# Writing the gated product of an expert block back into PSUM: one core, a chain of small gated MLPs in split fp32

## The reference

```
x = x + L0(x)                                   # linear + low-rank part
g, u = x @ gate_w, x @ up_w                     # layer 1, for 2 chosen experts and the shared one
x = x + sum_e weight_e * (gelu(g) * u) @ down_w
up, gate = x @ wu.T + bu, x @ wg.T + bg         # layer 2, one chosen expert
x = x + (silu(up) * gate) @ wd.T + bd
x = x + x @ w_bot.T + bias                      # layer 3, a mix of 8 matrices, masked
```

## Time and profile before

| | |
|---|---|
| three runs | 77.83, 78.18, 78.83 us, median 78.18 us |
| span of the profiled execution | 76.4 us from its first to its last instruction |
| TensorE busy | 70.4 us, 92% |
| VectorE busy | 58.6 us, 77% |
| ScalarE busy | 50.0 us, 65% |
| GpSimd busy | 46.3 us, 61% |
| granted TensorE clock | full speed in all 40 slices of the span |

### The profile page before, as it was taken

The page is one execution under the profiler, slowest core; times in us unless marked ns, Lnnn a source line. Parts: engine busy times, 40 slices in busy tenths (PEclk is TensorE's granted clock), DMA queues, the critical chain, the costliest instruction groups (busy, mean ns, idle before and its releaser), DMA issues.

```text
span 76.4 us, 1120 instructions
## 1 busy us (share of the span) xinstructions
PE 70.4 (92%) x303; PEld 54.1 (71%) x303; DVE 58.6 (77%) x93; ACT 50.0 (65%) x94; POOL 46.3 (61%) x48
## 2 busy tenths in 40 slices
PE   4949999799999899999999999999999999999950
PEld 4846788487877567778888788888788687684730
DVE  0165718996999999889987969669989969969940
ACT  5076749477675675577788776767977995736720
POOL 5020048308999999999999999999986300000000
PEclk9999999999999999999999999999999999999999
DMA  0679999999300000000000000000000000000034
GB/s 0 150 235 340 373 324 352 427 425 406 131 3 0 4 0 9 0 0 4 0 0 0 0 0 0 0 0 0 9 0 0 0 0 0 0 0 0 0 137 137
DMA packets 2740, 6.62 MB, mean 87 GB/s; under 512 B 432, under 2 KB 1456, under 8 KB 2736
## 3 DMA queue, kind: packets, MB, share of 16 engines
q1 hardware_dynamic: 2448, 6.18, 22.4%
q10 hardware_dynamic: 288, 0.39, 1.4%
HBM read 6.04 MB, written 0.52 MB: 86 GB/s over the span
## 4 chain that ended last, share of the span: by engine, by line
PE 81%; DVE 9%; DMA 4%; issue 2%; DVEq 0%
PE acc L414 10%; PE gp L410 8%; PE up L414 8%; PE up L410 8%; PE up L411 8%; PE gp L411 8%; PE gp L414 8%; PE acc L410 7%; PE acc L411 7%; DVE hlo L599 4%; DMA condb<-cond 4%; PE gp L521 1%; PE acc L406 1%; DVE wa L612 1%; PE acc L425 1%
## 5 line engine op out<-in xcount | busy, mean ns | idle before, releaser
L599 DVE TENSOR_TENSOR hlo<-h,hhi 128x512 fp32r<-128x512 f32 (+1 forms) x29 | 27.5, 948 | 1.0 <-ACT hhi L333 0.7
L346 ACT ACTIVATE act<-gp 128x512 f32<-128x512 f32 x24 | 14.4, 598 | 14.6 <-PE gp L414 13.3
L267 POOL TENSOR_TENSOR wlo<-raw_skill,whi 128x384 fp32r<-128x384 f32 x16 | 20.1, 1259 | 3.5 <-ACT whi L318 3.5
L333 ACT ACTIVATE hhi<-h 128x512 fp32r<-128x512 f32 (+1 forms) x29 | 17.7, 612 | 3.2 <-DVE h L584 2.6
L591 DVE SCALAR_TENSOR_TENSOR h<-up,gate_w,act 128x512 f32<-128x512 f32 x16 | 12.0, 749 | 4.6 <-ACT act L346 4.2
L414 PE MATMUL acc<-hlo,whi 128*128 128x512 f32 (+1 forms) x28 | 11.6, 415 | 1.0 <-DVE hlo L599 0.8
L410 PE MATMUL acc<-hhi,whi 128*128 128x512 f32 (+1 forms) x28 | 11.3, 402 | 0.0
L411 PE MATMUL acc<-hhi,wlo 128*128 128x512 f32 (+1 forms) x28 | 10.8, 387 | 0.0
L410 PE MATMUL gp<-xhi,whi 128*128 128x512 f32 x27 | 10.7, 397 | 0.1
L410 PE MATMUL up<-xhi,whi 128*128 128x512 f32 x27 | 10.7, 396 | 0.0
L411 PE MATMUL gp<-xhi,wlo 128*128 128x512 f32 x27 | 10.7, 395 | 0.0
(11 more groups left out here) (99 smaller groups left out, 99.3 us busy)
## 6 DMA issues: line engine op xcount, KB each, us to landing
raw_skill<-skill SPq DMA_DIRECT2D x4, 768.0 KB, 8.7
raw_l<-l SPq DMA_DIRECT2D x2, 386.5 KB, 9.2
raw_shared<-shared SPq DMA_DIRECT2D x4, 192.0 KB, 4.2
w3in<-l SPq DMA_DIRECT2D x1, 576.0 KB, 7.6
x<-x_t SPq DMA_DIRECT2D x2, 256.0 KB, 3.8
out_t<-res ACTq DMA_DIRECT2D x1, 256.0 KB, 2.1
params<-l SPq DMA_DIRECT2D x1, 128.0 KB, 2.6
out_t<-res ACTq DMA_DIRECT2D x1, 128.0 KB, 1.7
```

Source lines behind the costliest of these rows:

```text
L267: pool.tensor_tensor(wlo[:, p, :], raw_piece(p), whi[:, p, :], ALU.subtract).then_inc(s_wlo, 1)
L333: sc.activation(hhi[:, i, t], h[:, i, t], ACT.Copy).then_inc(s_hhi, 1)
L346: sc.activation(act[:, k % 2, :], gp[k % PAIRS][:, :], ACT.Gelu_apprx_tanh).then_inc(s_act, 1)
L599: ve.tensor_tensor(hlo[:, i, t], h[:, i, t], hhi[:, i, t], ALU.subtract).then_inc(s_hlo, 1)
```

## The change

The tile `h` goes away. `hidden(k)` writes its product over its own input, the up bank in PSUM, and both `h_hi(k)` and `h_lo(k)` read the product from there. Only the last block, whose halves overlap, keeps an SBUF tile (`h_last`). The up bank is therefore in use until `hlo` is made, so gate_up(k) waits for the low half of block k - 3 where it waited for its product, and the first half-wise down projection, which writes over a part of an up bank, waits likewise. `hidden(k)` no longer waits for the buffers of `h`.

```diff
-        h = sb("h", [P, HBUFS, T])
+        h_last = sb("h_last", [P, T])
...
+        def hidden_of(k, t):
+            return h_last[:, t] if k == N - 1 else up[k % PAIRS][:, t]
...
-                sc.activation(hhi[:, i, t], h[:, i, t], ACT.Copy).then_inc(s_hhi, 1)
+                sc.activation(hhi[:, i, t], hidden_of(k, t), ACT.Copy).then_inc(s_hhi, 1)
...
                 if k >= PAIRS:
-                    pe.wait_ge(s_h, k - PAIRS + 1)
+                    pe.wait_ge(s_hlo, k - PAIRS + 1)
...
                 if is_first(k):
-                    pe.wait_ge(s_h, N1 + 2)
+                    pe.wait_ge(s_hlo, N1 + 2)
...
             def hidden(k, t=slice(0, T)):
-                i = k % HBUFS
                 ve.wait_ge(s_act, k + 1)
                 ve.wait_ge(s_u, k + 1)
-                if k >= HBUFS:
-                    ve.wait_ge(s_hhi, k - HBUFS + 1)
-                    ve.wait_ge(s_hlo, k - HBUFS + 1)
-                a, u = act[:, k % 2, t], up[k % PAIRS][:, t]
+                a, u, out = act[:, k % 2, t], up[k % PAIRS][:, t], hidden_of(k, t)
...
-                    ve.tensor_tensor(h[:, i, t], u, a, ALU.mult).then_inc(s_h, 1)
+                    ve.tensor_tensor(out, u, a, ALU.mult).then_inc(s_h, 1)
...
-                ve.tensor_tensor(hlo[:, i, t], h[:, i, t], hhi[:, i, t], ALU.subtract).then_inc(s_hlo, 1)
+                ve.tensor_tensor(hlo[:, i, t], hidden_of(k, t), hhi[:, i, t], ALU.subtract).then_inc(s_hlo, 1)
```

More of the change, by code:

```diff
@@ L583, in hidden @@
                     c = L2_BLOCKS * PIECE + L2_BLOCKS + j
-                    ve.scalar_tensor_tensor(out=h[:, i, t], in0=u, scalar=raw_l2[:, b, c:c + 1], in1=a,
+                    ve.scalar_tensor_tensor(out=out, in0=u, scalar=raw_l2[:, b, c:c + 1], in1=a,
                                             op0=ALU.add, op1=ALU.mult).then_inc(s_h, 1)
                 elif expert_of(k) is None:
-                    ve.tensor_tensor(h[:, i, t], u, a, ALU.mult).then_inc(s_h, 1)
+                    ve.tensor_tensor(out, u, a, ALU.mult).then_inc(s_h, 1)
                 else:
@@ L590, in hidden @@
                     ve.wait_ge(s_rt, ROUTER_STEPS)
-                    ve.scalar_tensor_tensor(out=h[:, i, t], in0=u, scalar=gate_w[:, b, r:r + 1], in1=a,
+                    ve.scalar_tensor_tensor(out=out, in0=u, scalar=gate_w[:, b, r:r + 1], in1=a,
                                             op0=ALU.mult, op1=ALU.mult).then_inc(s_h, 1)
```

## The result

The changed kernel takes 75.78 us in the median of its first six runs (74.94 to 76.60); the kernel before, six runs beside them, 78.28 us. The measured ratio is 0.959, with an interval of 0.953 to 0.965, so about 75.1 us. Of the six runs of the changed kernel this ratio counts the three fastest, since the other three were over 1.5% above the fastest; that matters here, because its runs fall into a band from 74.9 to 76.6 us. The same kernel measured again, against newly measured runs of the kernel before, gave 0.970 (0.964 to 0.977, median 76.06 us) and 0.968 (0.962 to 0.974, median 76.07 us). Over all 16 runs its median is 76.0 us. So it is faster by 3 to 4%; the forecast of 75.9 us fits the middle of all runs, and the first measured ratio puts it just outside the range at its lower end.

A forecast was written before the change was run, and what follows sets the result against it. TensorE, busy 92% of the span, was taken to bound layer 1's loop, losing time waiting for low halves. Gains of 0.76 + 1.52 = 2.28 us off 78.18 gave 75.9 us, range 75.1 to 77.4.

The forecast's parts named there:

- What bounds the kernel, and the stretching: Layer 1's loop runs at TensorE's pace; low halves with two SBUF inputs are stretched while GpSimd works, up to 1843 ns.
- Rival C: Stretching has another cause than the SBUF inputs, so low halves from PSUM stay as long; 78.2 us, chance 0.07.
- hlo at 0.69 us: Low half reading PSUM and SBUF, in 27 of 28 blocks: takes 0.69 us, and 0.60 us to the next start.
- hlo(0), 0.76 us: Block 0's low half would end at 13.59 instead of 14.50, removing TensorE's wait before the third down matmul; gain 0.76 us.
- hlo(4) to hlo(7), 1.52 us: Blocks 4 to 7: VectorE's load falls to 2.09 us, just under TensorE's 2.10, so the waits go; gain 1.52 us.
- Rival B: Router steps at blocks 5 to 7 fall behind GpSimd instructions, returning about 0.9 us; 76.8 us, chance 0.14.
- The write into PSUM: Product written over its input in PSUM: costs 0; other end 0.55 us for a second pass over 512 elements.
- Rival D: Reading and writing one PSUM bank takes two passes, 0.55 us more a product; 79.3 us, chance 0.11.
- The high half from PSUM: ScalarE's copy reads PSUM, nearest row 598 ns against 626 from SBUF; under 0.1 us gain, counted as 0.
- GpSimd's lead: Weight pieces come no later relative to their start; least lead, at block 21, 3.8 us, with 1.5 us left at worst.
- Block 23 to 24, "Gain 0": The 0.26 us wait goes, but is lost behind ScalarE's table load, held by layer 2's `xlo` staying at 1.50 us.
- From the span to the median: Around the profiled span: the median of the runs was taken as 1.8 us above it.

The follow-up runs named there:

- block 21 alone: Kernel before with 32 warm-up matmuls, low half taking its first operand from PSUM in block 21 only; 77.36 us in one execution.
- block 20 alone: Kernel before with 32 warm-up matmuls, low half taking its first operand from PSUM in block 20 only; 77.66 us in one execution.
- blocks 19 to 21 together: Kernel before with 32 warm-up matmuls, low half taking its first operand from PSUM in blocks 19 to 21 only; median 77.52 us.

## Why the prediction was right or wrong

- **What bounds the kernel, and the stretching:** right. The low half is stretched because of its second SBUF operand while GpSimd works; taken alone that edit is the whole gain (75.30 against 75.22 us), and without it the rest of the change brings 0.36 us. Rival C is out.
- **hlo at 0.69 us:** 0.68 in every block; the nearest row gave it. The Trainium skill (VectorE: DVE Perf Modes, The TRN2 errata) gives a PSUM source a fixed part of 120 cycles and an SBUF source one of 58, by estimate 65 ns more; nothing of that is to be seen.
- **hlo(0), 0.76 us, with almost nothing to spare:** measured 0.77. The low half ended 0.08 us before the weight load at 14.48.
- **hlo(4) to hlo(7), 1.52 us:** measured 16.22 - 14.70 = 1.52 us. Rival B did not come about: the three router steps took 0.94, 0.16 and 0.95 us. In the second profile of the changed kernel they took 0.97, 1.10 and 0.85 us, and the blocks stayed 2.10 us apart as well.
- **The write into PSUM, 0 with 0.55 us as the other end:** 9 ns. Rival D is out. The high half from PSUM: 595 in place of 626 ns, as read.
- **GpSimd's lead:** it grew. The piece of block 21 was ready at 45.74 and used from 52.74, 7 us ahead, where the prediction had reckoned with 1.5 us at least.
- **Block 23 to 24, "Gain 0": wrong.** This is the step of the sum that failed. The 0.26 us stayed gained (from block 10 to block 24 it takes 0.23 us less), and from block 24 to VectorE's last step it takes another 0.05 us less (12.92 us in place of 12.97). The path was right: behind an unmoved table load the 0.26 us would have been lost, since block 25 starts 3.13 us after the load in the kernel before and in the run with block 21 alone. What failed is that the load would not move. The prediction said that `xlo` of layer 2 keeps two SBUF inputs and that "both it and its GpSimd neighbour move with the loop, so it stays". It went from 1.50 to 1.12 us. The changed kernel's rows around it:

```profile
55.07 0.68 DVE L598 TENSOR_TENSOR hlo<-up,hhi 128x512 fp32r<-128x512 f32 x1
55.22 1.01 POOL L270 TENSOR_TENSOR wlo<-raw_l,whi 128x384 fp32r<-128x384 f32 x1 [1.08 <-ACT whi L321]
55.66 1.12 DVE L623 TENSOR_TENSOR xlo<-x,xhi 128x512 fp32r<-128x512 f32 x1
```

and of the kernel before, GpSimd at the same place:

```profile
56.70 1.37 POOL L267 TENSOR_TENSOR wlo<-raw_l,whi 128x384 fp32r<-128x384 f32 x1 [0.22 <-ACT whi L318]
```

In both, `xlo` ends 0.54 or 0.55 us after GpSimd's piece does (58.61 after 58.07 before, 56.78 after 56.23 now). But the piece took 1.37 us before, for it waited in its turn for the low half of block 20, and 1.01 us now. With `xlo` the product of block 22 and, through ScalarE's queue, the table load come earlier, by about 0.4 us: the load starts 1.65 us after block 23 (58.59 and 56.94) in place of 2.05 us (60.44 and 58.39). Freeing block 20 alone brought the same (`xlo` 1.14 us, the load 0.35 us earlier), and blocks 19 to 21 together also the 0.26 us. The Trainium skill (SBUF — State Buffer, Who interferes with whom) calls the port pair that VectorE shares with GpSimd an exclusive lock; the chain low half, then GpSimd's piece, then `xlo`, each ending after the one before, agrees with that, and I had read the rule for one pair of instructions only.

- **From the span to the median: wrong in its range.** The prediction took 1.8 us for what lies around the span; it is 2.10 us in kernels with the tile `h` and 1.99 to 2.03 without it, and this 0.1 us of gain was in no term. It took one profile and the middle of the runs for one number, and did not see that TensorE's pace doubles at a moment that differed by 2.6 us between executions (8.0 to 10.6 us). Between the four profiles with 24 or 16 that moves the time by 1.2 us (75.37 to 76.60), most of the 1.7 us over which the runs of the changed kernel spread, and it explains how the first measured ratio, 0.959, could stand beside 0.970 and 0.968 later. The first result, 75.1 us, lies 0.8 us under the forecast: 0.3 to 0.4 us of it is the sum's error, the rest is that only its three fastest runs counted, which by the later profiles are those with an early step.
- **From the profile to the runs:** counted from the same place the two profiles differ by 2.6 us, with 32 warm-up matmuls the medians differ by 2.75 us, but with 24 by 2.3 us only. That the forecast of 75.9 us meets the 76.0 us of all 16 runs is therefore partly luck: a sum too small by 0.3 to 0.4 us met a start-up in which the changed kernel with 24 lost about as much against the kernel before. Why the kernel before gains less from the longer warm-up (0.3 us against 0.8 us) was not settled.

## What to carry over

Before an elementwise instruction's time is taken for its own, compare its shortest and longest rows, and ask whether GpSimd works beside the long ones and where both of its inputs lie: here one operand in PSUM took a stretched instruction from up to 1.84 us down to 0.68, and with it GpSimd's weight pieces from 1.35 to 1.02 us. When such an edit removes a lock between two engines, follow the lock through the neighbours too: the instruction that keeps its two SBUF inputs also gets shorter if the one it waits for was itself held up. And before comparing spans, look at the starts of the first matmuls for a step in pace: here its moment moved the same kernel by 1.2 us, where the change was worth 2.7 us.

## What was unexpected of the hardware

- TensorE's pace in the start-up doubles (0.21 to 0.11 us for 256 columns of fp32r) while the row of the granted clock shows full speed in all slices of it. The step came at 8.0 to 10.6 us in the five profiles in which TensorE had idled for 0.9 us or more before the first product, and before 4.8 us in six, by 6.4 us in all of the eleven with 32 or 40 warm-up matmuls, which left a gap of 0.3 us or less.
- A VectorE step of four elements a partition takes 0.15 us alone and up to 1.26 us beside GpSimd, also where it has one tensor input and a constant (`wa`: 0.97 us before, and in the profiles of the changed kernel either 0.16 us or 1.08 to 1.10).
- A VectorE product written over its own input in PSUM took 700 ns for 512 columns, against 691 ns with its output in SBUF: reading and writing one bank at once cost nothing worth counting.
